# A fused attention and mixture-of-experts layer: the eviction of each batch's query projection, one score step later on ScalarE

## What is computed

```
x = x + layernorm(attention(layernorm(x)))
x = x + layernorm(moe(layernorm(x)))

attention(x):
    c_kv = x @ W_DKV + b_DKV        # latent of 128 for keys and values
    c_q  = x @ W_DQ  + b_DQ         # latent of 128 for queries
    k_c, v_c, q_c = c_kv @ W_UK + b_UK, c_kv @ W_UV + b_UV, c_q @ W_UQ + b_UQ
    k_r, q_r = (x @ W_KR + b_KR) * pe, (x @ W_QR + b_QR) * pe
    16 heads of 32: softmax([q_c, q_r] [k_c, k_r]^T / sqrt(32)) @ v_c
    return ctx @ W_O + b_O
```

## Time and profile before

| | |
|---|---|
| median of 3 runs | 1496.23 us (1495.78 to 1498.4) |
| the profiled execution | 1495.43 us |
| its span in the profile | 1493.8 us |
| TensorE busy | 1455.7 us (97%) |
| VectorE busy | 1101.5 us (74%) |
| ScalarE busy | 872.9 us (58%) |
| GpSimd busy | 818.9 us (55%) |
| mean granted TensorE clock | 0.994 |

### The profile page before, as it was taken

One profiled execution on the slowest core, in us unless ns is written; L12 is line 12 of the kernel. 1 busy time (PEld: TensorE's weight loads), 2 busy tenths in 40 slices (PEclk: granted clock), 3 DMA queues, 4 the chain that ended last, 5 costly groups with the idle time before them and its releaser, 6 DMA issues.

```text
span 1493.8 us, 22671 instructions
## 1 busy us (share of the span) xinstructions
PE 1455.7 (97%) x7052; PEld 1035.4 (69%) x7052; DVE 1101.5 (74%) x2060; ACT 872.9 (58%) x1554; POOL 818.9 (55%) x808
## 2 busy tenths in 40 slices
PE   5999999999999999999999999999999999999998
PEld 3555656656666566666664588788888888878886
DVE  6778778777877787778778554871777777769888
ACT  5656466565575665655646555333666666685554
POOL 6477788786886977887859430003333322143342
PEclk9899999999999999999999999999999999999999
DMA  7678599496795995976965421546987788797774
GB/s 187 82 105 160 70 194 164 85 179 125 123 211 72 180 174 74 192 140 106 223 104 125 142 80 67 178 160 187 348 242 227 229 237 230 244 331 241 225 240 160
DMA packets 162766, 255.59 MB, mean 171 GB/s; under 512 B 20052, under 2 KB 70356, under 8 KB 160596
## 3 DMA queue, kind: packets, MB, share of 16 engines
q1 hardware_dynamic: 143336, 202.62, 59.6%
q0 software_dynamic: 12864, 41.96, 9.8%
q10 hardware_dynamic: 6448, 9.57, 1.8%
HBM read 103.87 MB, written 58.46 MB: 109 GB/s over the span
## 4 chain that ended last, share of the span: by engine, by line
PE 84%; DVE 6%; issue 2%; DMA 2%; ACT 2%; POOL 2%; SPq 0%; DVEq 0%; POOLq 0%; ACTq 0%
PE bank L117 17%; PE bank L831 10%; PE bank L899 9%; PE bank L853 9%; PE bank L745 8%; PE bank L734 7%; PE bank L764 7%; PE bank L753 7%; PE bank L773 2%; POOL a L1908 1%; PE bank L685 1%; PE bank L683 1%; PE bank L684 1%; DVE a L1086 1%; PE bank L911 1%
## 5 line engine op out<-in xcount | busy, mean ns | idle before, releaser
L1908 POOL TENSOR_TENSOR a<-a 128x512 f32<-128x512 f32 x376 | 489.0, 1329 | 92.8 <-ACT a L1654 55.3
L1654 ACT ACTIVATE a<-bank 128x512 f32<-128x512 f32 x512 | 296.7, 597 | 254.4 <-PE bank L753 214.8
L1086 DVE TENSOR_REDUCE a<-bank 128x1 f32<-128x512 f32 x512 | 321.4, 681 | 47.0 <-PE bank L734 44.3
L745 PE MATMUL bank<-a 128*128 128x512 f32 x512 | 216.7, 423 | 6.6 <-ACT a L1654 6.3
L753 PE MATMUL bank<-a 68*128 68x512 f32 x512 | 203.6, 398 | 1.0 <-DVE a L1098 0.9
L853 PE MATMUL bank<-c 128*128 128x512 f32 x768 | 177.4, 390 | 1.3 <-DVE c L1172 0.7
L117 PE MATMUL bank<-a 128*128 128x512 f32 x666 | 177.6, 400 | 0.3 <-DVE a L1061 0.3
L831 PE MATMUL bank<-c 128*128 128x512 f32 x768 | 177.3, 390 | 0.6 <-ACT c L1696 0.5
L734 PE MATMUL bank<-a 128*128 128x512 f32 x496 | 171.9, 412 | 2.1 <-DVE a L1086 0.7
L745 PEld LDWEIGHTS bank<-a 128*128 128x128 f32 x512 | 96.6, 189 | 103.1 <-ACT a L1654 57.9
L831 PEld LDWEIGHTS bank<-c 128*128 128x128 f32 x768 | 143.7, 188 | 32.7 <-issue 1.7
(11 more groups left out here) (236 smaller groups left out, 2258.4 us busy)
## 6 DMA issues: line engine op xcount, KB each, us to landing
a<-a SPq DMA_DIRECT2D x262, 256.0 KB, 8.2
yp_scratch<-f SPq DMA_DIRECT2D x79, 256.0 KB
f<-f SPq DMA_DIRECT2D x256, 64.0 KB
a<-in_L_attn_x SPq DMA_DIRECT2D x15, 1024.0 KB, 7.4
x_scratch<-a SPq DMA_DIRECT2D x8, 1024.0 KB, 4.7
h_scratch<-a SPq DMA_DIRECT2D x8, 1024.0 KB, 9.6
hT_scratch<-s SPq DMA_DIRECT2D x8, 1024.0 KB, 9.1
c<-hT_scratch SPq DMA_DIRECT2D x8, 1024.0 KB, 7.1
```

Source lines behind the costliest of these rows:

```text
L745: e.matmul(SC[n % 2][:], K.Kc[z][:, j, i * P:(i + 1) * P], K.Qc[z][:, j, :], start=True, stop=False)
L1086: e.tensor_reduce(K.mx[:, i, j:j + 1], K.MX[n % 3][:], AX.X, ALU.max).then_inc(Z.max, 1)
L1654: e.activation(K.pt[:, n % NP, :], K.SC[n % 2][:], ACT.Exp, scale=SCALE).then_inc(Z.exp, 1)
L1908: e.tensor_tensor(K.acc[:, j, :], a, K.pt[:, n % NP, :], ALU.add).then_inc(Z.acc, 1)
```

## The change

ScalarE's part of `("proj", b + 1, "q")` gets a stage name of its own, `"proj high"`, which only ScalarE knows. It is put at `n = 24` in the class behind the score tile that stands at 24. So ScalarE first takes the exponential of tile (3, 0) and then evicts the projection. TensorE's, VectorE's and SyncE's parts stay where they were. The keys' projection and batch 0's query projection keep their place on ScalarE too: seven evictions move.

```
@@ beside_order
     elif g == 1:
         if b + 1 < B:
             put("proj", [("proj", b + 1, w) for w in ("kv", "q")])
+            at.append(((32 * u + 24, 1), ("proj high", b + 1, "q")))
         if b:
             put("y", norm_order("y", b - 1))
@@ scalar_program
     def proj(b, what):
-        if what == "r":
-            return
+        if what == "kv" or (b, what) == (0, "q"):
+            proj_high(b, what)
+
+    def proj_high(b, what):
         bank = begin("proj", b, what)
         n, bias_ = (0, K.bdkv) if what == "kv" else (1, K.bdq)
         w.wait_ge(Z.w1b, 8 * 16)
...
-    stages = {..., "proj": proj, "v": v, ...
+    stages = {..., "proj": proj, "proj high": proj_high, "v": v, ...
```

More of the change, by code:

```diff
@@ L1842, in finish @@
                      scale=K.crw[:, z, 4, 0:1]).then_inc(Z.cn, 1)
-    stages = {"split w": split_w, "round": round_, "scale": scale, "turn": turn, "proj": proj, "v": v, "v part": v_part, "half": half, "half parts": half_parts, "plant": plant, "stack": stack, "scores": scores, "keep": keep,
+    stages = {"split w": split_w, "round": round_, "scale": scale, "turn": turn, "proj": proj, "proj high": proj_high, "v": v, "v part": v_part, "half": half, "half parts": half_parts, "plant": plant, "stack": stack, "scores": scores, "keep": keep,
               "turn2": turn2, "route": route, "split h": split_h, "split up": split_up, "round up": round_up, "round down late": round_down_late,
```

## The result

| | before | after |
|---|---|---|
| median of 22 runs each | 1495.73 us (1493.25 to 1499.2) | 1498.65 us (1496.92 to 1502.08) |
| ratio | | 1.0020, 95% interval 1.0015 to 1.0026 |
| the profiled execution, its span | 1495.43, 1493.8 us | 1499.79, 1498.2 us |
| granted TensorE clock | 0.994 | 0.994 |

The change costs 2.9 us; the interval is 2.2 to 3.9 us. The two profiled spans lie 4.4 us apart, more than the medians do, so the spans alone are no good measure. The trace gives a better one, used throughout: TensorE's sums of the exponentials (`total`) mark the first and the last unit of the attention. The first answer is the kernel before, the second the changed one; behind the count stand the durations in ns (least, median, most), then the first and last start in us.

What follows compares the result with a forecast made beforehand. TensorE, busy in 97% of the span, was taken to bound the kernel. Four places at 0.52 (2.08) plus 0.30 gave +2.38 us on 1496.23: 1498.6 us, own range 1498.0 to 1499.2, overall range 1496.4 to 1501.2.

Steps and rivals of the forecast that it cites:

- The gain: ScalarE's exponential of score (3,0) starts 0.12 us earlier, and so does TensorE's stalled score (3,2).
- step 5: TensorE's fifth `top` of the next unit, released by VectorE's second maximum, starts 0.52 us late, the earlier exponential included.
- The eviction: On ScalarE the moved eviction starts 0.48 us after the exponential starts, at 292.42 instead of 291.48: 0.94 us late.
- ScalarE behind it: Exponential (3,1) starts at 293.00, not 292.54; the values' matmuls hide it with 0.64 us to spare; even after three exponentials.
- L1022 0.94 late: VectorE's low part of the query projection and everything behind it start 0.94 us late; the first maximum 0.69 us late.
- The bound that placed it at or behind that end: If a maximum starts at the aggregates' end or 0.03 behind, each of five places costs 0.12 more: +3.0 us.
- The end of the debt: At VectorE's next transposition, now waiting 0.67 us for TensorE, VectorE arrives 0.69 later, TensorE 0.52 later: VectorE just fits.
- The seven places: Moved evictions, units 1, 5, 9, ..., 25: 0.52 us each at 2, 3, 4, 6; 0.30 at 5; none at 1, 7.
- Rival B: Only the 0.12 us earlier exponential is felt, at four places: -0.5 us; chance 0.12.
- C: Neither VectorE's nor TensorE's slack holds; the whole 0.94 us passes at six places, seen at the `top` matmuls: +5.6 us; chance 0.20.
- E: The added gaps on TensorE drop its clock to half at five places: +18 us; chance 0.03.
- D: The eviction's place doesn't matter; gain and debt cancel: 0 us; chance 0.10.

Runs made afterwards that it cites:

- the kernel whose ScalarE order is changed and whose cost is gone: The changed kernel with VectorE's first three h statistics put ahead of its query projection part; ratio to the kernel before 1.0002, attention 772.4 us, -0.1 against before.

## Why the prediction was right

The median moved by 2.9 us to 1498.65; I had 1498.6, from a sum of +2.38. That the two medians agree within 0.1 us is luck in part: the three runs that I started from have a median 0.5 us above that of the 22, and the measured change is 0.5 us above the sum. The attention's length, where the sum can be checked without the other stages' scatter, moved by 2.4, and that is what bears the prediction out. By the steps:

1. The gain: the score behind the exponential came 0.12 us nearer to the projection, as computed. Right; and in the changed kernel it is worth nothing, as step 5 said. The prediction did not see that it has a second bound in front of it: at places 2, 5 and 6 the first `top` now waits 0.30, 0.47 and 0.27 us for the landing of SyncE's copy, where it waited 0.20, 0.36 and 0.16.

2. The eviction: 0.94 us late by the working, 1.38 − 0.43 = 0.95 measured, 0.50 behind the exponential.

3. ScalarE behind it: the values' matmuls hid the later exponential (score (3,3) starts 1.66 behind (3,2) in both kernels). Shown also by the kernel whose ScalarE order is changed and whose cost is gone.

4. VectorE: L1022 0.94 late. The first maximum starts 0.08 before the aggregates' modelled end (296.36 against 296.44), as the earlier trace rows had it. The bound that placed it at or behind that end falls away.

5. The fifth `top`: 0.17 behind the second maximum by the working. It came 0.15 behind it, and 6.90 behind the projection, against 6.93 foretold. The weight load waited for a maximum twice, for the fourth and for the fifth `top`. I had named only the fifth, but the fourth's wait is contained in it.

6. The end of the debt: the transposition waits 0.63 us for TensorE, before 0.67. So VectorE is in time again, as said, but "just fits" was a misreading: by the working's own numbers 0.67 − 0.69 + 0.52 = 0.50 us of waiting were left.

Two numbers in the prediction's text are wrong without touching its sum. Place 3 is unit 9, projecting for batch 3, and the copies named in step 6 are those of unit 12; the places as listed (units 1, 5, 9, ...) and all the rows are right.

The seven places came out as 0, 0.62, 0.52, 0.47, 0.36, 0.48 and 0.05. The spread of 0.15 among the four like ones was not foreseen; the sum was. At place 2 the fifth `top` is 0.43 us later against the projection, 0.46 to 0.49 at its likes; the rest of its 0.62 comes in the unit behind, in steps too small to name. Rival B is refuted by the waits in front of the `top` matmuls, C by the size of about 0.5 us a place, E by the granted clock, D by the interval. The chances said 0.63 for within 0.2% and 0.35 for slower than that; the ratio of 1.0020 stands on the border between the two, with its interval on both sides.

What stays open: 2.9 us on the medians against 2.4 in the attention. The interval of 2.2 to 3.9 us covers both, and nothing was tried on the other 0.5. The stretch behind the attention can't decide it: it is 650 us long before and 653 after, and in the other traces it lies between 647 and 654 with no order.

## What to carry to other kernels

When an instruction moves one place back on an engine that has time, look for the engine that waits for its result, and at what stands in that engine's queue behind the wait: here four statistics, their aggregates and the maxima, and TensorE behind those. A delay costs what is left of it after each slack on the way (0.94 − 0.25 − 0.17 = 0.52), so the timeline of one place, with the slack read in front of each waiting instruction, gives the price of the whole; and places that look alike in the code (here 1, 5 and 7) may have other slack. Work that needs no result of the wait belongs ahead of it: three statistics ahead of the waiting instruction took the whole cost away. And before a gain on the critical engine is counted, look for the next thing it waits for: an idle time of 0.2 us in front of a weight load, which the view puts down to no one, was the landing of a copy, and it took a part of what three of the kernels above had gained.

## What the runs showed that I had not expected

A program so tightly planned stands on several bounds at once: the last copy for a unit lands some 12.1 us after its issue and meets the first `top` of the next unit, which waits for it by up to 0.2 us at four places and 0.36 and 0.89 at two, beside a wait for an exponential and a backlog on VectorE. Taking the wait for the exponential away brought the landing to light (+0.7 instead of -2.5 us). The 12.1 us are no property of a copy of 256 KB: with the copies two steps earlier it is 8.8. Why was not looked for.

A TensorE wait costs more than the page's idle time says. The matmul group of the row at 292.40 is called idle for 0.21 us, but its matmul starts 0.61 behind the one ahead (291.79), where 0.23 is the distance in a stream, and the next one comes 0.34 behind it, again for 0.23: about 0.5 us in all.
